# Four edits in one to the fused attention and routing kernel: when energies wait, how x, the heads and x2 are turned, where their low halves are made, and which engine squares the heads

## The reference

```
x = x + 0.5 * ffn(layernorm(x))       # route: top 256 of 4096 rows for each of 16 experts
x = x + attention(layernorm(x))       # differential attention, 16 heads of 32, 4 key heads
x = x + 0.5 * ffn(layernorm(x))

attention: q, k, v = x@Wq, x@Wk, x@Wv;  q, k = rope(q), rope(k)
  scores = softmax(causal(q.k)/sqrt(32))          # two score maps per head, a = 0 and 1
  diff   = softmax(causal(scores[0] - lam*scores[1]))
  att    = diff @ v;  att = att * rsqrt(mean(att*att) + eps) * rms_w * 0.2
  return att @ Wo
ffn: logits = x@Wr + b;  S = softmax(logits);  G, idx = top_k(S.T, 256)
  y[idx] += G * (x[idx] @ We + be)
```

## Time and profile before

| | us |
|---|---|
| median of three runs | 2129.94 |
| profiled execution, its own time | 2123.43 |
| its span, first to last instruction | 2121.7 |
| PE busy | 1555.5 (73%) |
| DVE busy | 1467.3 (69%) |
| ACT busy | 1219.2 (57%) |
| POOL busy | 1057.3 (50%) |

### The profile page before, as it was taken

One profiled execution on the slowest core, in us unless ns is written; L12 is line 12 of the kernel. 1 busy time (PEld: TensorE's weight loads), 2 busy tenths in 40 slices (PEclk: granted clock), 3 DMA queues, 4 the chain that ended last, 5 costly groups with the idle time before them and its releaser, 6 DMA issues. The chain is left out here.

```text
span 2121.7 us, 44318 instructions
## 1 busy us (share of the span) xinstructions
PE 1555.5 (73%) x10713; PEld 1091.9 (51%) x10713; DVE 1467.3 (69%) x4351; ACT 1219.2 (57%) x3332; POOL 1057.3 (50%) x1477
## 2 busy tenths in 40 slices
PE   0579814347888888988888888888888888886521
PEld 0355402125666666666666666666666566763221
DVE  5774431127887888888888888888888776751167
ACT  0121102126887878887888887788878776761100
POOL 0220003225666667767766777767677565552200
PEclk9999956666878999899999999999999877676655
DMA  3330271111111111111111121111111100000084
GB/s 122 94 87 0 67 245 30 41 39 33 24 28 36 41 48 43 38 51 47 45 48 38 43 52 43 49 43 38 49 48 42 40 20 20 15 15 30 35 324 158
DMA packets 183784, 122.58 MB, mean 58 GB/s; under 512 B 140225, under 2 KB 140609, under 8 KB 183746
## 3 DMA queue, kind: packets, MB, share of 16 engines
q1 hardware_dynamic: 183746, 122.15, 19.6%
HBM read 57.07 MB, written 33.55 MB: 43 GB/s over the span
## 5 line engine op out<-in xcount | busy, mean ns | idle before, releaser
L1185 ACT ACTIVATE ex<-bank,nbias 128x512 f32<-128x512 f32 (+3 forms) x1024 | 527.8, 534 | 141.2 <-DVE nbias L902 140.7
L895 DVE TENSOR_REDUCE nmax<-bank 128x2 f32<-128x1024 f32 (+3 forms) x448 | 340.7, 795 | 29.9 <-PE bank L1331 29.5
L1361 PEld LDWEIGHTS bank<-vs,pr 128*128 128x128 f32 x2560 | 343.2, 210 | 17.8 <-issue 13.4
L1361 PE MATMUL bank<-vs,pr 128*128 (+1 forms) x2560 | 343.4, 286 | 7.2 <-issue 4.1
L1329 PE MATMUL bank<-ks,qs 96*128 (+2 forms) x1024 | 271.8, 342 | 95.7 <-ACT ex L1185 94.2
L1343 PE MATMUL bank<-cst,df 128*128 128x128 f32 x1280 | 274.5, 319 | 88.8 <-ACT pr L1202 88.5
L1081 POOL TENSOR_SCALAR ex<-ex,gam 128x128 f32<-128x128 f32 (+3 forms) x512 | 313.4, 623 | 0.0
L1202 ACT ACTIVATE pr<-bank 128x128 f32<-128x128 f32 (+3 forms) x512 | 233.0, 455 | 70.5 <-PE bank L1343 70.1
L927 DVE CUSTOM_DVE_ANT_0 df<-ex 128x128 f32<-128x128 f32 (+3 forms) x512 | 263.3, 529 | 9.7 <-issue 4.9
L1343 PEld LDWEIGHTS bank<-cst,df 128*128 128x128 f32 x1280 | 174.1, 171 | 117.9 <-ACT pr L1202 101.6
L1185 ACT ACTIVATION_READ_ACCUMULATOR ex<-bank,nbias 128x1 f32 x1024 | 216.6, 212 | 0.0
(11 more groups left out here) (215 smaller groups left out, 3164.0 us busy)
## 6 DMA issues: line engine op xcount, KB each, us to landing
qs<-turned SPq DMA_DIRECT2D x384, 64.0 KB, 2.2
xs<-in_x SPq DMA_DIRECT2D x64, 256.0 KB, 3.0
x_dram<-y SPq DMA_DIRECT2D x32, 256.0 KB, 3.8
b_xs<-x_dram SPq DMA_DIRECT2D x32, 256.0 KB, 2.6
x<-x_dram SPq DMA_DIRECT2D x32, 256.0 KB, 2.7
x_dram<-x SPq DMA_DIRECT2D x32, 256.0 KB, 2.0
y_dram<-scratch SPq DMA_DIRECT2D x32, 256.0 KB, 2.0
c_x<-x_dram SPq DMA_DIRECT2D x8, 1024.0 KB, 13.6
```

What stands on the lines that cost most here:

```text
L895: ins = dve.tensor_reduce(nmax[:, j, i, :], energy(j, i), X, ALU.max, negate=True)
L1185: ac.activation(ex[j % 4][:, a, lo:hi], energy(j, i)[:, a, :], ACT.Exp, bias=nbias[:, j, i, a:a + 1], scale=reg, accum_out=esum[:, j, i, a ...
L1361: mm = pe.matmul(bank[:, 7, t * DV:(t + 1) * DV], pr[j % 2][:, lo + k * P:lo + (k + 1) * P], val, start=(k == 0), stop=(k == t))
```

## The change

The energies of the longer tile now wait bank by bank: the first map for the last exponential of step j - 2, the second for the first exponential of step j - 1. The shorter tile's energies wait for the second one. In every fourth step a function `order` swaps the two maps of the longer tile, on PE and ACT, so that the bank needed first comes first.

x, the heads and x2 are turned in fp32, by four transposes and not eight. ACT copies the turned bank to fp16 (that is the high half, 512 columns), and DVE subtracts this from the bank and writes the low half. The three casts on ACT ahead of the turn, and the three subtractions on POOL, are gone. The square of the attention output moves from POOL (L1151) to ACT. The load of the next x tile waits for the turn, and no longer for the low half.

```diff
-                        if i == 1:
-                            exp_done.wait(pe, at.units(4, 1 - 4))
+                        if i == 0:
+                            exp_done.wait(pe, at.units(4, 1 - 4))
+                        for k, a in enumerate(order(j, i)):
+                            if i == 1:
+                                exp_done.wait(pe, at.units(4, (3 - 8, 0 - 4)[k]))
...
-                def turn(pair_, cols, done):
-                    for a in range(2):
-                        for k in range(KT):
-                            tr = pe.transpose(pair_[:, a, k * P:(k + 1) * P],
-                                              split[:, a, cols.start + k * P:cols.start + (k + 1) * P], ident_h[:, :])
+                def turn(to, rows, done):
+                    for k in range(KT):
+                        tr = pe.transpose(to[:, k * P:(k + 1) * P], rows[:, k * P:(k + 1) * P], ident)
...
-                    ac.copy(xt[:, :, :], prep_pair).then_inc(xt_out.sem, 1)
+                    ac.copy(xt[:, 0, :], prep_bank).then_inc(hi_done.sem, 1)
...
+                def low(src, dst, hi, lo):
+                    def f(u):
+                        hi.wait(dve, u)
+                        dve.tensor_tensor(dst[:, 1, :], src, dst[:, 0, :], ALU.subtract).then_inc(lo.sem, 1)
...
+                def square(tau, u):
...
+                    ac.activation(squares[:, :].rearrange("p (h d) -> p h d", h=H),
+                                  att[:, ds(u & 7, 1), :, 0:D].rearrange("p a h d -> p (a h) d"),
+                                  ACT.Square).then_inc(sq_done.sem, 1)
...
-                           {1: [prep(take_x)], 5: [high_heads], 7: [rope_high(0)], 8: [post(take_heads)],
-                            10: [prep(take_chunks(0))], 12: [rope_high(1)], 13: [high2], 15: [prep(values)],
+                           {1: [square, prep(take_x)], 7: [prep(rope_high(0)), post(take_heads)],
+                            10: [prep(take_chunks(0))], 12: [prep(rope_high(1))], 15: [prep(values)],
```

More of the change, by code:

```diff
@@ L731, in program @@
             post_bank = bank[:, 5, :]
[L732 removed]
+            prep_bank = bank[:, 4, :]
             spread = [False, False]
@@ L801, in span, with order @@
                 return (0, first) if i == 0 else (first, PAIR)
+            def order(j, i):
+                return (1, 0) if i == 1 and j % 4 == 1 else (0, 1)
             def energy(j, i):
@@ L818, in load @@
                 def load(u):
-                    lo_done.wait(sp, u - 1, apart_s)
+                    xt_done.wait(sp, u - 1, apart_s)
                     sp.dma_start(xs[:, :], flat(x1_t[ds(u, 1), :, :])).then_inc(x_in, 16)
@@ L1114, in rope_add @@
                     return f
-                def low(u):
-                    hi_done.wait(gp, u)
-                    gp.tensor_tensor(split[:, 1, ROWS], xn[:, :], split[:, 0, ROWS], ALU.subtract)\
-                      .then_inc(lo_done.sem, 1)
                 def rope_low(n):
@@ L1159, in _ @@
                 run_bodies(gp, [[(5, shift)], [(2, mask), (2, scale)], []],
[L1160 to L1164 removed]
+                           {2: [post(head_root)], 7: [prep(rope_add(0))], 8: [prep(rope_low(0))], 11: [prep(rope_add(1))],
+                            14: [post(root2), prep(rope_low(1))], 15: [prep(rope_add(2))], 19: [prep(rope_low(2))]},
+                           {18: [root]},
                            [(rope_add(0), 0), (rope_low(0), 0), (root, 1), (rope_add(1), 0), (rope_low(1), 0), (rope_add(2), 0),
[L1166 to L1167 removed]
+                            (rope_low(2), 0)], spread,
+                           [(root2, 0), (head_root, 1)])
             @blk.scalar
             def _(ac):
[L1171 to L1172 removed]
+                for s in (hi_done, rhi_done, v_done, turned_out, exp_done, shifted_long, prob_done, ah_done, hi2_done,
+                          y_out, sq_done):
                     s.start(ac)
@@ L1183, in f @@
                         lo, hi = span(j, i)
-                        for a in range(2):
+                        for a in order(j, i):
                             ac.activation(ex[j % 4][:, a, lo:hi], energy(j, i)[:, a, :], ACT.Exp,
@@ L1263, in take_x2 @@
                     o_done.wait(ac, u)
-                    ac.copy(xt2[:, :, :], post_pair).then_inc(xt2_out.sem, 1)
+                    ac.copy(xt2[:, 0, :], post_bank).then_inc(hi2_done.sem, 1)
+                def square(tau, u):
+                    if u is None:
+                        return
+                    att_out.wait(ac, (u >> 2) * H + (H - 1))
+                    squares = rot if spread[1] else asq
+                    if not spread[1]:
+                        ac.wait_ge(y2_st, u * 16 + 16)
+                    rope_done.wait(ac, 3 * (tau if tau is not None else NT) - 1)
+                    rlo_done.wait(ac, 3 * (tau if tau is not None else NT) - 1)
+                    ac.activation(squares[:, :].rearrange("p (h d) -> p h d", h=H),
+                                  att[:, ds(u & 7, 1), :, 0:D].rearrange("p a h d -> p (a h) d"),
+                                  ACT.Square).then_inc(sq_done.sem, 1)
                 def take_chunks(n):
@@ L1388, in turn_x @@
                         turned_out.wait(pe, 3 * u - 1)
-                    lo_done.wait(pe, u)
-                    turn(prep_pair, ROWS, xt_done)
+                    xn_done.wait(pe, u)
+                    lo_done.wait(pe, u - 1)
+                    turn(prep_bank, xn, xt_done)
                 def project(n):
@@ L1395, in f @@
                     def f(u):
-                        xt_out.wait(pe, u)
+                        lo_done.wait(pe, u)
                         if spread[0] and n == 2:
@@ L1430, in turn_heads, with product_o @@
                     y_out.wait(pe, u - 1)
+                    an_done.wait(pe, u)
+                    turn(post_bank, an, ant_done)
+                def product_o(u):
                     al_done.wait(pe, u)
-                    turn(post_pair, HEADS, ant_done)
-                def product_o(u):
-                    at_out.wait(pe, u)
                     three(pe, post_bank, *parts(at, wo_h, wo_l, 0, E)).then_inc(o_done.sem, 1)
@@ L1439, in turn_x2, with route @@
                     x2_done.wait(pe, u)
+                    xn2_done.wait(pe, u)
+                    turn(post_bank, xn2, xt2_done)
+                def route(u):
                     lo2_done.wait(pe, u)
-                    turn(post_pair, HEADS, xt2_done)
-                def route(u):
-                    xt2_out.wait(pe, u)
                     three(pe, post_bank[:, 0:NX], *parts(xt2, wr_h, wr_l, 0, NX)).then_inc(route_done.sem, 1)
```

104 lines of the change are left out of this document (25 added, 79 removed).

## The result

The changed kernel takes 2166.97 us (median of 4 runs, 2165.08 to 2170.29) against 2126.03 for the kernel before beside it: ratio 1.0194, 95% interval 1.0163 to 1.0225, so it is slower. The forecast was 2110, with a range of 2062 to 2150; sign and range were both wrong. A few single executions at a much lower granted clock, such as one of 2214.97 us at 0.741 of the kernel with the square alone, are left out of all ratios. The profiled execution's span is 2168.5 us, 46.8 more than before.

The account below looks back on a forecast made before the run. DVE's list was taken as the path of full bodies, except from step 6's scaling to `take_head`. Terms 10 - 7 - 8 - 8 - 2.5 = -15.5 us gave 2108, or 2114 against the median; forecast 2110, range 2062 to 2150.

Parts of the forecast that it names:

- Steps 0 and 1: Full bodies: DVE's wait for the square and x's low half, less the head roots' wait and shorter scaling: +1.2 us.
- The low half of the heads: Steps 2 to 5 of a full body: DVE's 1.4 us hidden in its 1.45 us wait for PE, so 0.
- Step 5: Full bodies: a shorter row scaling, -0.72 us, against 0.2 of waiting and 0.69 of work for x2's low half: +0.2.
- The energies: Steps 6 and 7 of a full body: PE's work up to `take_head` starts sooner with the new waits: -0.9 us.
- bound of -1.6: Far bound of the energies' gain in steps 6 and 7, us a body, if that stretch's half clock goes too.
- bound of -0.35: Near bound of the energies' gain in steps 6 and 7, us a body: PE's wait alone goes.
- Stretching: Small DVE operations lengthened by POOL's: beyond two places on the path counted as 0; bound 4.5 us a body saved.
- Bodies K = 0 to 4: The five bodies at the start: part of PE's waits for exponentials comes back, -1.3 us each, -7 us together.
- The six at the end: Six bodies after the full ones: 2.5 us of waits back, less 1.2 for the square's wait, each: -8 us together.
- The last four tiles: Sequential tiles at the end: casts, subtractions and part of the copy go, DVE's low halves come: -8 us.
- The five tiles alone: Five tiles at the start, paced by stacking DMAs: only ACT's cast ahead of its last copy goes, -2.5 us.
- Rival (a): Full bodies: DVE becomes the later one in every step and pays for all, +2.1 us a body; chance 0.24.

Follow-up runs that it names:

- late heads: The changed kernel with the low half of the heads moved one slot later, behind the row maxima of step 3: 2166.18 us, ratio 1.0177.
- none: The changed kernel without DVE's three subtractions and its waits for ACT's copies; PE takes the high half for the low one: 2104.73 us, ratio 0.9906.
- work alone: The kernel "none" with three DVE operations of 128x512 on constants at the subtractions' places, nobody waiting for them: 2156.65 us, ratio 1.0155.
- filled: The changed kernel with three more copies of the first energy matmul of each step's longer tile: 2160.63 us, ratio 1.0168.

## Why the prediction was wrong, point by point

The ends of DVE's row scalings divide a body. Means over the 21 full bodies, with the prediction's terms put to the same places (its -0.72 for the row scaling of step 5 and -0.2 for that of step 0 belong to the stretches that these scalings end):

| from the scaling of | before, us | now, us | change | forecast |
|---|---|---|---|---|
| step 0 to step 2 | 10.98 | 13.04 | +2.1 | +1.4 |
| step 2 to step 5 (low half of the heads) | 17.53 | 17.94 | +0.4 | -0.7 |
| step 5 to step 6 (low half of x2) | 4.84 | 5.64 | +0.8 | +0.9 |
| step 6 to step 0 (energies, `take_head`) | 11.76 | 11.16 | -0.6 | -1.1 |

- **Steps 0 and 1, +1.2 a body: the parts right, the sum not.** The head sums wait 1.15 us for the square (forecast 1.2), x's low half takes 0.69 and waits for nothing, the wait for the head roots is gone. But the stretch grew by 0.6 us more than that, as the row scaling at its end takes 1.15 us in the mean where it took 0.24. The square's part is 0.95 (alone) to 1.22 (in the changed kernel).
- **The low half of the heads, 0: the step that failed.** It failed in size: the wait is 2.0, not 0.7, since POOL, relieved of 1.16 us, now meets the row scaling. And it failed in kind: "from here to step 5 DVE has the 1.45 us of waiting for PE" took a wait as room for work and put 1.4 us at nothing. That wait fell by only 0.6 us, and where the work was put back by itself it stood at 42.5/21 = 2.0 us; the three operations then cost 2.59 us a body for their 2.05. The wait itself is another matter: without it (the late heads) the body was no shorter, and the long scaling is also in the kernel "none" above, whose body is 45.19. So the runs lay the main cost on DVE's added work, and not on the long scaling; the waits by themselves cost 0.82.
- **Step 5, +0.2: one part read from a single body.** x2's low half takes 0.69 and waits 0.1, as forecast. But the scaling of 0.95 us, from which -0.72 was taken, is in 12 of 21 bodies; the other nine have 0.23. The mean falls from 0.64 to 0.29, so -0.35 was there to gain.
- **The energies, -0.9 a body: wrong in the mean, and it hangs on the clock.** PE's wait fell by 1.5 us a body and `take_head` waits 2.2 (forecast under 1.8). The kernel with this edit alone gained nothing in full bodies in the mean. From the end of the row scaling of step 6 to `take_head` it is 8.46 us in the body shown (1248.65 to 1257.11) and was 8.72 before (1208.92 to 1217.64). Windows of 6.6 us that begin 1.5 us or so ahead of it, now and before; the last numbers are PEclk, DMA share, GB/s:

```profile
1247.00:1253.60 6.60, 6.26 (x40) 4.02 (x41) 6.31 (x18) 4.91 (x14) 3.82 (x8) 0.50 0.00 0
```

```profile
1207.20:1213.80 6.60, 5.54 (x49) 4.24 (x47) 6.31 (x19) 6.60 (x17) 4.57 (x9) 0.75 0.00 0
```

  The gain was 0.3 and not 0.9, with PE at half clock there for longer (0.50 against 0.75). Where the clock was full, this stretch took 7.1 to 7.2 us, which is the prediction's bound of -1.6, "if the half clock of this stretch goes too". No kernel with the old wait had full clock there, so how much of this is the wait and how much the clock is not shown. And in the kernel with extra matmuls the body was no shorter for it. The bound of -0.35, "the wait alone", was no bound: it held only for PE and not for the body.
- **Stretching: its total was underrated and its place missed.** The three small DVE operations took 55.5 + 83.4 + 48.8 = 187.7 us before (L902, L915, L936) and 157.9 now, -1.4 us a body of the 4.5 that POOL gave up. The Trainium skill, in "SBUF — State Buffer" (Terms), has DVE and GpSimd exclude each other on a shared port pair; the rows at 1223 agree, with 1.19 against 0.23. But L904 takes 0.6 us a body more, ahead of ACT's whole chain. That what was freed lay mostly beside other waits is argued, not shown.
- **Bodies K = 0 to 4, -7: +8.8.** The energies' waits alone account for +10.4; the granted clock falls with them but is not the whole of it, as above. **The six at the end, -8: +2.2.** Alone, the energies' waits give +2.6 there, the square +3.9 and the turns 0.1, and the same code moves by 3 us; only the missing gain of 8 is clear. DVE's two low halves stood in no term of this sum, without a reason. The kernels without the subtractions do not show them as the cost: 259.5 us without the work, 257.0 with it.
- **The last four tiles, -8: -19.3.** Direction right, size too small. The new turns with DVE's low halves give -11.7 alone, the square on top of them 7.5 more. By itself, beside the old turns, the square gives no gain there (117.4 us against 114.9). The five tiles alone, -2.5: -2.5; kernels with the same new turns lie between 155.4 and 158.1 us there, so a match to 0.1 is luck.

Together 56.2 + 8.8 + 2.2 - 19.3 - 2.5 = +45.4 us, where the spans differ by 46.8. Rival (a) named the mechanism: "DVE pays for all of it", +2.1 us a body; it was 2.7. Its reason against, that both of DVE's waits lie behind new work, was the reason that misled.

What stays open is why the body takes the same 47.74 to 47.79 us in five kernels of different content (changed, without the energies' waits, late heads, work alone, filled), and 51.2 in another. The edits are not additive here, by up to 3.6 us a body, and no sum of terms can be trusted below that.

## What to carry to other kernels

A wait in a list that feeds its own releaser may be latency and not slack: here work put ahead of it did not shrink it. Count new work of the engine that closes the loop in full until a run shows it hidden, and read the length of an operation from all bodies, not from one. When an engine that shares something with the path loses work, ask which operation of the path it will now meet. A change that gains in a sequential stretch and loses in a coupled one is to be applied by stage: here that made +1.9% into -0.6%.

## What the runs showed of the hardware

- A DVE subtraction PSUM minus SBUF of 128x512, written as fp16, takes 0.69 us, and this also where POOL has a 128x512 operation of 1.16 us under way. With both operands constants in SBUF it takes 0.68, and 1.27 beside the same POOL operation.
- Four fp32 128 x 128 transposes take 0.60 us at full clock (L1342 in the changed kernel), no more than eight fp16 ones (0.61).
- With the energies' new waits the granted clock is 0.75 and not 0.80 in bodies K = 0 to 4; PE's busy time is higher by 15 us where its wait is lower by 14. Extra matmuls that raised the clock to 0.81 did not shorten the phase.
